# Gate of the last block: logits and turned rows taken from x before the norm, scaled afterwards

## The reference

```python
def _L1_ffn_ref(x, gate_w, gate_b, weight1, weight2):      # x: (8 images, 256 tokens, 32 channels)
    logits = jnp.einsum('bsd,ed->bse', x, gate_w) + gate_b # 16 experts
    probs = jax.nn.softmax(logits, axis=1)                 # over the 256 tokens
    vals, idx = jax.lax.top_k(probs.transpose(0, 2, 1), K) # K = 8 tokens for each expert
    ...
    gathered = jnp.take_along_axis(x, flat_idx[:, :, None], axis=1)
    ...
    pooled = jnp.einsum('bked,bke->bed', gathered, topv)
    ...
    h = jax.nn.gelu(jnp.einsum('ebd,edh->ebh', h, weight1), approximate=False)
    ...
    out = jnp.einsum('ebh,eho->ebo', h, weight2)
    ...
    outputs = outputs.at[jnp.arange(Bn)[:, None], flat_idx].add(weighted)

def _ln_t(v, eps=1e-05):
    m = jnp.mean(v, axis=-1, keepdims=True)
    s = jnp.var(v, axis=-1, keepdims=True)
    return (v - m) / jnp.sqrt(s + eps)
...
t = t + _L1_ffn_ref(_ln_t(t), ...)
```

## Time and profile before

| | us |
|---|---|
| median of 3 runs | 134.95 |
| their range | 134.52 to 134.99 |
| the profiled execution | 134.91 |
| its span in the profile | 133.0 |
| PE busy | 119.0 (89%) |
| DVE busy | 72.5 (54%) |
| ACT busy | 68.3 (51%) |
| POOL busy | 24.6 (18%) |

### The profile page before, as it was taken

The page is one execution under the profiler, slowest core; times in us unless marked ns, Lnnn a source line. Parts: engine busy times, 40 slices in busy tenths (PEclk is TensorE's granted clock), DMA queues, the critical chain, the costliest instruction groups (busy, mean ns, idle before and its releaser), DMA issues.

```text
span 133.0 us, 3161 instructions
## 1 busy us (share of the span) xinstructions
PE 119.0 (89%) x1212; PEld 84.0 (63%) x1213; DVE 72.5 (54%) x147; ACT 68.3 (51%) x121; POOL 24.6 (18%) x32
## 2 busy tenths in 40 slices
PE   6969889998989899999795899999999987989891
PEld 5546566668323325488784778988888976656650
DVE  0189985428452342204999969789595004346142
ACT  3453795278230402402997996987956651347000
POOL 8994000007600000000434205014000000000000
PEclk9999999999999999999999999999999999999958
DMA  3544000000101000000000000000000000000002
GB/s 114 150 72 97 0 0 5 0 0 10 30 0 25 8 7 2 0 0 5 0 0 5 0 0 5 0 5 0 0 7 0 5 0 2 0 5 0 0 5 84
DMA packets 2653, 2.16 MB, mean 16 GB/s; under 512 B 1290, under 2 KB 2346, under 8 KB 2632
## 3 DMA queue, kind: packets, MB, share of 16 engines
q0 software_dynamic: 464, 0.67, 2.6%
q1 hardware_dynamic: 1736, 0.65, 1.9%
q10 hardware_dynamic: 432, 0.55, 1.2%
HBM read 1.60 MB, written 0.26 MB: 14 GB/s over the span
## 4 chain that ended last, share of the span: by engine, by line
PE 58%; DVE 21%; ACT 9%; issue 6%; DMA 2%; SPq 2%; DVEq 0%; ACTq 0%
PE ps L493 9%; PE ps L962 9%; DVE smat L898 5%; PE ps L976 4%; PE ps L986 4%; PE ps L486 3%; PE ps L1275 3%; PE ps L286 3%; ACT tx L833 2%; DMA bvrow<-in_L_conv_bv 2%; DVE smatT L719 2%; PE ps L510 2%; PE ps L506 2%; PE ps L636 2%; PE ps L498 2%
## 5 line engine op out<-in xcount | busy, mean ns | idle before, releaser
L898 DVE TENSOR_TENSOR smat<-ty,tx 128x1536 f32<-128x1536 f32 (+1 forms) x14 | 21.5, 1555 | 4.3 <-ACT tx L833 4.3
L939 ACT ACTIVATE smatT<-ps 128x1536 f32<-128x1536 f32 x12 | 17.4, 1452 | 7.8 <-PE ps L962 7.7
L962 PE MATMUL ps<-cst,smat 128*128 128x128 f32 x144 | 18.1, 275 | 2.6 <-DVE smat L898 2.3
L962 PEld LDWEIGHTS ps<-cst,smat 128*128 128x128 f32 x144 | 15.7, 140 | 4.3 <-DVE smat L898 3.2
L486 PE MATMUL ps<-cst 128*128 128x256 f32 x44 | 12.6, 399 | 0.0
L493 PE MATMUL ps<-cst 128*128 128x512 f32 x26 | 12.1, 604 | 0.0
L986 PE MATMUL ps<-samp,wc 128*128 128x128 f32 x72 | 11.0, 291 | 0.0
L976 PE MATMUL ps<-smatT,xt 128*32 128x96 f32 x384 | 10.4, 249 | 0.3 <-ACT samp L930 0.3
L986 PEld LDWEIGHTS ps<-samp,wc 128*128 128x128 f32 x72 | 8.9, 190 | 1.6
L815 POOL TENSOR_SCALAR disty<-disty 128x288 f32<-128x288 f32 x3 | 6.3, 2088 | 17.2 <-ACT disty L822 17.2
L976 PEld LDWEIGHTS ps<-smatT,xt 128*32 128x32 f32 x384 | 7.9, 109 | 2.3 <-issue 1.8
(11 more groups left out here) (195 smaller groups left out, 193.0 us busy)
## 6 DMA issues: line engine op xcount, KB each, us to landing
cst<-in_cst ACTq DMA_DIRECT2D x1, 278.0 KB, 3.8
x<-in_x SPq DMA_DIRECT2D x2, 128.0 KB, 3.2
ew<-in_L_ffn_weight POOLq DMA_DIRECT2D x4, 64.0 KB, 2.3
ew<-in_L_ffn_weight POOLq DMA_DIRECT2D x1, 256.0 KB, 4.3
cst<-in_cst ACTq DMA_DIRECT2D x1, 129.0 KB, 3.2
w<-in_L_ffn_ffn_w SPq DMA_DIRECT2D x2, 64.0 KB
out<-fin SPq DMA_DIRECT2D x1, 128.0 KB, 1.7
out<-fin ACTq DMA_DIRECT2D x1, 128.0 KB, 1.8
```

Of the source, the lines that this page charges most:

```text
L898: return nc.vector.tensor_tensor(smat[:, n % 3, BP * part.start:BP * part.stop, :].rearrange("p u (g r c) -> p (u g) r c", g=DG, c=W), ty[ ...
L939: nc.scalar.activation(smatT[:, n % 2, :, :, :].rearrange("p k g n -> p (k g n)"), ps[:, bank:bank + 3, :].rearrange("p b n -> p (b n)"), ...
L962: last = nc.tensor.transpose(ps[:, bank + u // BP, (u % BP) * P:(u % BP + 1) * P], smat[:, n % 3, u, :], ident)
```

## The change

The gate's weights are centred once: VectorE takes from each expert's weights their mean over the channels (three small operations on `gw_n`, placed before the second norm), so that weights times x equals weights times the centred x. The logits are then made from x itself, before any variance is known, and once instead of twice. The factor 1/sqrt(variance) comes afterwards, in the logits' own rows. New constants `rows0` and `rows1` (128x128 each, loaded by GpSimd) let TensorE write the variance of each row's image in that row (L1355). ScalarE makes `rrow` of it, and VectorE makes `lg` = (logits + shift term) x `rrow` (L1546). The turned rows come from x too: a matmul with x as weights and `center` as data, and a second one that adds the shift (L1363, L1365). Their factor is the small tile `rtok` of 128x16. Eight narrow records (L1359) and two ScalarE operations make it, and VectorE multiplies it in while it moves the rows to `ut` (L1559). ScalarE copies `pmT` in VectorE's place. In the fillers, the one behind the variances is gone, two short ones of 128 columns (`keep_short`) are new, and two stand behind L1400 instead of one. SyncE waits for both stores.

```diff
+            dve.wait_ge(sem("ld_c"), 64)
+            link(nc.vector.tensor_reduce(gwm[:, :], gw_n[:, :], AX.X, ALU.add))
+            link(nc.vector.tensor_scalar(gwm[:, :], gwm[:, :], 1.0 / C, None, ALU.mult))
+            nc.vector.tensor_scalar(gw_n[:, :], gw_n[:, :], gwm[:, 0:1], None, ALU.subtract).then_inc(sem("c_gw"), 1)
...
+            pool.dma_start(cst[:, NLAST:], dr("cst")[:, NLAST:]).then_inc(sem("ld_d"), 16)
...
-            norm_act(act, 4, eps5, bn[:, 8:9])
+            for j in range(J):
+                act.wait_ge(sem("norm_c"), J * 3 + j + 1)
+                nc.scalar.activation(sq[:, j * N:(j + 1) * N], ps[:, CBANK[j], 0:N], ACT.Square,
+                                     bias=bn[:, 8:9]).then_inc(sem("norm_sq"), 1)
+
+            def deviations(out, var, count):
+                act.wait_ge(sem("e_var"), count)
+                nc.scalar.activation(out, var, ACT.Ln, bias=eps5).then_inc(sem("e_dev"), 1)
+                act.wait_ge(sem("e_dev"), 2 * count - 1)
+                nc.scalar.activation(out, out, ACT.Exp, scale=-0.5).then_inc(sem("e_dev"), 1)
+
+            deviations(rrow[:, :], ps[:, 3, 0:N], 1)
+            deviations(rtok[:, :], ps[:, 0, 0:J * NH * BP], 2)
             act.wait_ge(sem("e_max"), 1)
...
-            act.wait_ge(sem("e_ut"), 1)
-            nc.scalar.activation(ut[:, :, :].rearrange("p i c -> p (i c)"), ps[:, 1, :], ACT.Copy).then_inc(sem("e_uts"), 1)
+            act.wait_ge(sem("e_sel"), 1)
+            nc.scalar.activation(pmT[:, :, :].rearrange("p h n -> p (h n)"), ps[:, 3, 0:NH * P],
+                                 ACT.Copy).then_inc(sem("e_pmts"), 1)
...
-                norm_pe(pe, 4, lambda j: (sem("c_xn"), j + 1), 2, 4, shift)
+                gates = [gwt[:, j, :, :, :].rearrange("p e g j -> p (e g j)") for j in range(J)]
+                shift = bn[:, 7:8]
+
+                pe.wait_ge(sem("c_xn"), 1)
+                nc.tensor.matmul(ps[:, CBANK[0], 0:N], center, x[:, 0:N], start=True, stop=True).then_inc(sem("norm_c"), 1)
+                pe.wait_ge(sem("c_stat"), 3)
+                nc.tensor.matmul(ps[:, 5, 0:1], center, shift, start=True, stop=True)
                 for j in range(J):
...
+                    last = nc.tensor.matmul(ps[:, 5, 1:2], gates[j], shift, start=(j == 0), stop=(j == J - 1))
+                last.then_inc(sem("c_fold"), 1)
+                pe.wait_ge(sem("c_xn"), 2)
+                nc.tensor.matmul(ps[:, CBANK[1], 0:N], center, x[:, N:], start=True, stop=True).then_inc(sem("norm_c"), 1)
+                for j in range(J):
+                    last = nc.tensor.matmul(ps[:, 2, 0:N], gates[j], x[:, j * N:(j + 1) * N],
+                                            start=(j == 0), stop=(j == J - 1))
                 last.then_inc(sem("e_lg"), 1)
+                pe.wait_ge(sem("ld_d"), 16 * 10)
                 for j in range(J):
...
+                    pe.wait_ge(sem("norm_sq"), J * 3 + j + 1)
+                    last = nc.tensor.matmul(ps[:, 3, 0:N], const("rows%d" % j), sq[:, j * N:(j + 1) * N],
+                                            start=(j == 0), stop=(j == J - 1))
+                last.then_inc(sem("e_var"), 1)
                 for i in range(J * NH):
-                    last = nc.tensor.transpose(ps[:, 1, i * P:(i + 1) * P], u[:, i * P:(i + 1) * P], ident)
+                    last = nc.tensor.matmul(ps[:, 0, i * BP:(i + 1) * BP], sq[:, i * P:(i + 1) * P], meanm[:, ::C],
+                                            start=True, stop=True)
+                last.then_inc(sem("e_var"), 1)
+                for i in range(J * NH):
+                    nc.tensor.matmul(ps[:, 1, i * P:(i + 1) * P], x[:, i * P:(i + 1) * P], center,
+                                     start=True, stop=False)
+                    last = nc.tensor.matmul(ps[:, 1, i * P:(i + 1) * P], shift.broadcast_to([P, P]), center,
+                                            start=False, stop=True)
                 last.then_inc(sem("e_ut"), 1)
...
+                keep_short(1, 1)
                 pe.wait_ge(sem("e_in"), 2)
...
+                keep_short(1, 1)
                 pe.wait_ge(sem("e_hid"), 1)
...
-                keep_clock(1, 1)
+                keep_clock(2, 1)
```

On VectorE, the copy from bank 5 takes two columns instead of one, and behind it:

```diff
-            for j in range(J):
-                centered, scale = norm_dve(dve, 4, j)
-                nc.vector.scalar_tensor_tensor(out=u[:, j * N:(j + 1) * N], in0=centered, scalar=bn[:, 8:9], in1=scale,
-                                               op0=ALU.add, op1=ALU.mult).then_inc(sem("e_u"), 1)
-
             dve.wait_ge(sem("e_lg"), 1)
-            link(nc.vector.max(ltop[:, :], ps[:, 0, 0:N]))
+            dve.wait_ge(sem("e_dev"), 2)
+            link(nc.vector.scalar_tensor_tensor(out=lg[:, :], in0=ps[:, 2, 0:N], scalar=bn[:, 9:10], in1=rrow[:, :],
+                                                op0=ALU.add, op1=ALU.mult))
+            link(nc.vector.max(ltop[:, :], lg[:, :]))
```

More of the change, by code:

```diff
@@ L81, in constants @@
     cols["repl"] = p[:, None] % C == p[None, :] % C
+    for j in range(J):
+        cols["rows%d" % j] = ((p[:, None] // C == p[None, :] // J % BP) & (p[None, :] % J == j)) / C
     at, off = {}, 0
@@ L123, in metaformer_kernel @@
         cst = sb("cst", [P, NCST])
-        NFIRST = CA["eps"][1]
+        NFIRST, NLAST = CA["eps"][1], CA["rows0"][0]
         def const(name):
@@ L197, in metaformer_kernel @@
         agg = sb("agg", [P, 2])
-        bn = sb("bn", [P, 9])
+        bn = sb("bn", [P, 10])
         ebcol = sb("ebcol", [E, E * B])
         gw_n = sb("gw_n", [E, C])
+        gwm = sb("gwm", [E, 1])
+        lg = sb("lg", [P, N])
+        rrow = sb("rrow", [P, N])
+        rtok = sb("rtok", [P, J * NH * BP])
         gwt = sb("gwt", [P, J, E, BP, J])
@@ L493, in keep_long, with keep_short @@
                 nc.tensor.matmul(ps[:, bank, :], meanm, cst[:, 0:2 * N], start=True, stop=True)
+        def keep_short(n, bank):
+            for _ in range(n):
+                nc.tensor.matmul(ps[:, bank, 0:P], meanm, cst[:, 0:P], start=True, stop=True)
         def keep_warm(n, bank):
@@ L1232, in _ @@
             act.wait_ge(sem("out_ready"), 2)
-            act.dma_start(out[:, N:], fin[:, N:]).then_inc(sem("stored2"), 16)
-            act.wait_ge(sem("stored2"), 16)
+            act.dma_start(out[:, N:], fin[:, N:]).then_inc(sem("stored"), 16)
         @block.tensor
@@ L1320, in to_end @@
+                pe.wait_ge(sem("c_xn"), 2)
+                nc.tensor.matmul(ps[:, CBANK[1], 0:N], center, x[:, N:], start=True, stop=True).then_inc(sem("norm_c"), 1)
+                for j in range(J):
+                    last = nc.tensor.matmul(ps[:, 2, 0:N], gates[j], x[:, j * N:(j + 1) * N],
+                                            start=(j == 0), stop=(j == J - 1))
                 last.then_inc(sem("e_lg"), 1)
+                pe.wait_ge(sem("ld_d"), 16 * 10)
                 for j in range(J):
-                    last = nc.tensor.matmul(ps[:, 2, 0:N], gwt[:, j, :, :, :].rearrange("p e g j -> p (e g j)"),
-                                            u[:, j * N:(j + 1) * N], start=(j == 0), stop=(j == J - 1))
@@ L1470, in _ @@
             by_fit(dve, fit_dve, wide_dve)
[L1472 removed]
+            dve.wait_ge(sem("ld_d"), 16 * 10)
             dve.wait_ge(sem("c_out"), 1)
```

30 lines of the change are left out of this document (13 added, 17 removed).

## The result

| | before | after |
|---|---|---|
| median, us | 134.86 | 134.16 |
| lowest and highest of 20 executions each | 134.38 to 135.26 | 133.83 to 134.66 |
| profiled execution, us | 134.91 | 134.12 |
| its span, us | 133.0 | 132.3 |

The ratio is 0.9958 (95%: 0.9947 to 0.9968). The gain of 0.6 to 0.7 us is real and about half of the 1.25 forecast, and at 0.4% it lies within the 0.5% bound. The range of the forecast holds it, the likeliest case's own range (to 134.0) doesn't. That the range holds it is luck: it reaches that far for case 2, and the clock did not fall.

A forecast was written before the change was run, and what follows sets the result against it. The gate's time is one thread handed between engines, none a bottleneck; the end pays about 0.9 us for the low clock. 134.91 - 1.26 (0.86 from the clock) = 133.65, by the median 133.7; range 133.2 to 135.1.

The forecast's parts named there:

- the likeliest case: The clock stays at full level to the end: 133.7 us, own range 133.3 to 134.0, chance 0.53.
- case 2: The clock falls near the end as before: 134.6 us, or 135.05 if 0.5 earlier; chance 0.27.
- The path to the maximum: Gate, from the shift matmuls to VectorE's maximum: 0.36 us earlier; ScalarE copying pmT earns 0.04 more.
- Pace of TensorE: Matmul records with changing weights step at 0.12 us each, for wide and narrow data alike: the loads set it.
- Case 4: TensorE's weight loads do not hide, 0.24 instead of 0.12 per added or narrow record: 137.0 us, chance 0.08.
- TensorE just in time for pm: TensorE, behind the variances, is free at 121.23 and pm ready at 121.27: fits by 0.04 us, costs nothing.
- Case 3: TensorE is late with pm at 0.14 per record; the path's gain is lost, the end's stays: 134.1 us, chance 0.12.
- The inputs in SBUF: Maximum and match_replace read SBUF instead of PSUM: given nothing; the skill's rule would give 0.13 us less.
- Edits at nothing: gw_n operations (some 0.6 us) and GpSimd's extra load (about 1 uncovered) lie in idle time or waits: no cost.
- The end: Output matmuls take 1.13 at full clock; second fin at 129.05 against 130.31: 1.26 us in all, 0.86 from the clock.
- Case 1: The granted clock stays full through the output matmuls: 133.7 us, own range 133.3 to 134.0, chance 0.53.

The follow-up runs named there:

- the early edits: Before plus three VectorE operations centring gw_n, a TensorE wait for them and one more 128 KB GpSimd load; 134.93 us, ratio 1.0007.
- the same nine profiles: Profiles with the branch at the end, both stores and a held clock; a store's packets are spread over 0.66 to 1.28 us.
- the control: After run once more, unchanged, as base for the branch and store runs on the same chip; 134.12 us, ratio 0.9924 to before.

## Why the prediction was half right

**The path to the maximum** (forecast 0.36, with pmT 0.40). The mechanism held, and one factor for both halves does away with the second Ln, Exp and u. It measured 0.20 at the maximum and 0.25 at the selection. The narrow records cost the squares 0.47 (115.60 - 0.13 - 115.00) where 0.48 were counted. The missing 0.16 are small pieces: the variances ended at 117.63 - 0.13 = 117.50 instead of 117.45, and the maximum came 0.65 behind Exp's end where I had put 0.55. It takes 0.13 from Exp's end to lg's start and 0.04 from lg's end to the maximum, which the forecast covered with 0.07. By itself the part is worth 0.22 in time (134.84 to 134.62), with the caveat above.

**Pace of TensorE** (forecast 0.12 per record). 0.11 for the 16 records of the turned rows and about 0.10 for the eight of 4 columns. Case 4, loads that do not hide, is out. The rule of the Trainium skill, page TensorE: Matmul & The Clock Gate, section The mechanism, that a load runs beside matmuls only when the row group differs, does not hold here: all these records use all rows, and L1363's and L1365's 0.30 for two loads lie beside the matmuls.

**TensorE just in time for pm** (forecast: fits by 0.04). It fits by about 0.26, as pm is ready at 121.57 and the filler's last step ends near 121.31. Case 3 did not come in after; the run with the variances first, where TensorE is 0.34 later, brought it.

**The inputs in SBUF.** MAX8 took 0.43 and match_replace 0.41 from SBUF, as from PSUM before. The 0.13 by the Trainium skill, page VectorE: DVE Perf Modes, section on the TRN2 errata, isn't seen.

**Edits at nothing.** Right: the early edits measured nothing, `ut` (0.68) was done at 122.16, ahead of pmT at 122.47, and the table load (1.28) ended at 123.77, 2.4 ahead of Gelu. The short fillers at 124.52 and 125.98 ended before their successors were due.

**The end.** This is the step that failed: "**1.26 in all**, of which 0.86 comes from the clock", with "the span's last 2.2 us are issue and landing, unchanged; I allow 0.1 either way". Case 1 came true. The clock held in all 27 executions of after, and the last addition came 1.05 earlier (1.18 on the common count). But two things were wrong about what that is worth.

1. The last 2.2 us were not unchanged. I followed the end only through the instructions that compute and the stores. TensorE's branch over the arm that does not run lasts 3.35 to 3.9 us from the issue of the output matmuls, and stores that meet its fetch land later. In before it was over at 131.74, and the late additions held the span to 133.00. In the same nine profiles the span ends 0.49 to 0.52 behind the branch. By that count it could not end before about 132.2 (an estimate, 131.74 + 0.5), so some 0.8 was all that could be earned while the branch stayed where it was. Now branch and landings, together, set the end. They take back 0.35 in time (the control against the kernel without the branch) and 0.67 in the two profiled tails (3.34 against 2.67). In the profiled executions: 1.18 earned, 0.13 lost to a later start of the program, 0.33 to the tail, which leaves the 0.72 of the spans.
2. The 0.86 was read from one profiled execution in which the clock fell. At the second addition it is right (0.93 in the profile of the new fillers alone). But the clock falls in 51 of 83 executions, and those where it does not are 0.28 faster already. The median of before stands for a mixture.

Without the branch the fillers are worth 0.65; with it 0.23. Those 0.23 and the path's 0.22 make 0.45, and the whole change measured 0.63 against before in its own groups. The rest of 0.18 is within two of its standard errors (0.13), and I leave it open, as I do why before gains 0.19 without its branch in the executions whose clock fell (134.86 to 134.67), though its profile shows the branch over 1.2 ahead of the end.

## What to carry to other kernels

Follow the end past the last useful instruction: the last branch of each engine, what it fetches, and the landing of the stores. A gain just ahead of it is worth only the distance to the next of these. A stall read from one profile needs its frequency: the mean clock of every execution of the kernel before would have told that the fall comes in 6 of 10. And where two engines hand work to each other with 0.3 us of slack, moving work forward on one can cost more than it earns.

## What the runs showed of the hardware

- TensorE's branch over the arm that does not run takes 3.35 to 3.9 us at the end of the program. Moved to its middle it takes 3.44 and leaves the engine without work for 4.18 us. The branches of VectorE and ScalarE on the same line, over arms of their own, take 63 and 50 ns.
- With an instruction fetch of 16 KB beside it, a store of 128 KB lands in 2.0 to 2.5 us instead of 1.7 to 1.8.
- The start of the program is not the same in each profile: the convolution's statistics begin between 110.25 and 111.13 in kernels that are nearly alike up to there, later where the granted clock first rises later (4.1 us in before, 6.6 to 7.4 in those that are 0.4 to 0.8 late). A difference of that size in one profile is no result.
- Matmul records that each follow a weight load of their own took 0.10 to 0.11 each, whether the data had 4 columns (eight records) or 128 (sixteen).
